# A routed feed-forward layer on one core: two-slot loops, weight pieces spread over four slots, row loads moved from SP to POOL

## The reference

```python
x = x + jnp.tanh(g_xattn[0]) * xattn(ctx_512, layernorm(x), W, b)   # 0.6*sigmoid(si+sj+b) + 0.4*layernorm(x)
# ffn: xt = layernorm(x) as (4096, 1024); W is (8, 1024, 1024), b is (8, 1024)
logits = xt @ wg
probs = jax.nn.softmax(logits, axis=-1)
idx = jnp.argmax(probs, axis=-1)
gate = jnp.take_along_axis(probs, idx[:, None], axis=1)
expert_out = jnp.einsum('nh,eoh->neo', xt, W) + b[None, :, :]
out = jnp.einsum('ne,neo->no', one_hot(idx) * gate, expert_out)
x = x + jnp.tanh(g_ffn[0]) * out
```

## Time and profile before

| | us |
|---|---|
| median of 3 runs | 683.54 |
| lowest, highest | 682.17, 690.35 |
| span of the profiled execution | 687.3 |

### The profile page before, as it was taken

How to read it: one execution, slowest core, us unless ns; L and a number is a source line. 1 busy time by engine, 2 the same in 40 slices (tenths; PEclk the granted TensorE clock), 3 DMA queues, 4 the chain that set the end, 5 groups by cost and what they waited for, 6 DMA issues and landing times.

```text
span 687.3 us, 14019 instructions
## 1 busy us (share of the span) xinstructions
PE 576.6 (84%) x2841; PEld 461.2 (67%) x2842; DVE 445.2 (65%) x557; ACT 274.1 (40%) x408; POOL 331.8 (48%) x489
## 2 busy tenths in 40 slices
PE   7898889888707969979779997995999799699990
PEld 5576667666505848858567885884888588588870
DVE  3357778697699885856784587588378557843420
ACT  2367766686424333413333333333343233333220
POOL 1446777788623336325336533633633364356540
PEclk8569999999957989989989998997999899899995
DMA  7911577576679876764776497577756656545530
GB/s 262 403 40 33 175 261 237 198 217 223 239 258 259 238 214 190 225 208 152 224 220 196 147 243 213 189 219 215 217 168 204 189 166 198 164 132 186 182 126 13
DMA packets 83666, 134.72 MB, mean 196 GB/s; under 512 B 11568, under 2 KB 64304, under 8 KB 83504
## 3 DMA queue, kind: packets, MB, share of 16 engines
q1 hardware_dynamic: 73712, 99.47, 49.4%
q0 software_dynamic: 9792, 33.82, 12.8%
HBM read 99.44 MB, written 35.91 MB: 197 GB/s over the span
## 4 chain that ended last, share of the span: by engine, by line
PE 27%; DVE 23%; issue 19%; ACT 9%; POOL 7%; DMA 6%; DVEq 3%; POOLq 2%; ACTq 2%; SPq 1%
PE pair L1058 12%; DVE wt L782 7%; PE pair L985 4%; DVE xr L718 4%; ACT wt L598 4%; DVE pair L777 4%; PE pair L996 3%; PE pair L969 3%; PE pair L974 3%; ACT rb L617 2%; DVE rows L804 2%; DMA out_x<-rows,scatter_row 2%; DMA rows<-table 1%; DVE xc_tr L725 1%; POOL out_x L500 1%
## 5 line engine op out<-in xcount | busy, mean ns | idle before, releaser
L1058 PE MATMUL pair<-wt,xt 128*128 x1728 | 416.2, 404 | 62.6 <-DVE rows L804 41.6
L1058 PEld LDWEIGHTS pair<-wt,xt 128*128 128x128 f32 x1728 | 336.9, 196 | 141.5 <-issue 66.5
L488 POOL TENSOR_TENSOR rows<-rows,rb 128x1024 f32<-128x1024 f32 x37 | 88.7, 2398 | 164.2 <-ACT rb L617 162.6
L782 DVE TENSOR_TENSOR wt<-pair,wt 128x1024 f32 (+1 forms) x64 | 77.5, 1212 | 32.7 <-ACT wt L598 32.7
L598 ACT ACTIVATE wt<-pair 128x1024 f32 (+1 forms) x64 | 64.2, 1024 | 77.7 <-DVE pair L777 70.1
L604 ACT ACTIVATE xt<-pair 128x1024 fp32r<-128x1024 f32 x38 | 39.0, 1026 | 133.0 <-DVE pair L790 110.6
L777 DVE STREAM_TRANSPOSE pair<-w_raw 128x1024 f32<-128x1024 f32 x64 | 79.7, 1250 | 1.9
L790 DVE STREAM_TRANSPOSE pair<-xb 128x1024 f32<-128x1024 f32 x38 | 47.7, 1255 | 46.5 <-issue 26.3
L804 DVE SCALAR_TENSOR_TENSOR rows<-pair,scal,rows 128x1024 f32<-128x1024 f32 x36 | 46.0, 1278 | 44.6 <-PE pair L1058 44.2
L617 ACT ACTIVATE rb<-bias_bc,scal 128x1024 f32 (+1 forms) x37 | 46.0, 1244 | 48.4 <-POOL scal L485 41.1
L794 DVE TENSOR_TENSOR xt<-pair,xt 128x1024 fp32r<-128x1024 f32 x38 | 46.4, 1221 | 28.1 <-ACT xt L604 25.9
(11 more groups left out here) (123 smaller groups left out, 417.9 us busy)
## 6 DMA issues: line engine op xcount, KB each, us to landing
w_raw<-in_L_ffn_W SPq DMA_DIRECT2D x256, 128.0 KB
xb<-table SPq DMA_DIRECT2D x156, 128.0 KB
rows<-table SPq DMA_DIRECT2D x38, 520.0 KB
xr<-in_x SPq DMA_DIRECT2D x32, 512.0 KB, 6.9
ctx_in<-in_ctx SPq DMA_DIRECT2D x8, 512.0 KB, 4.9
bias_bc<-in_L_ffn_b SPq DMA_DIRECT2D x8, 512.0 KB
out_x<-rows,scatter_row POOLq DMA_INDIRECT x36, 4.2
table<-xr,pos POOLq DMA_INDIRECT x32, 4.5
```

Of the source, the lines that this page charges most:

```text
L488: nc.gpsimd.tensor_tensor(rows[:, k, 0:H], rows[:, k, 0:H], rb[:, :], ALU.add).then_inc(base_ready, 1)
L782: nc.vector.tensor_tensor(where[:, :, 1].rearrange("p a k o -> p (a k) o"), ps[:, :].rearrange("p (k o) -> p k o", k=K), where[:, :, 0].re ...
L1058: last = nc.tensor.matmul(out_ps[r % 2][:, HALF * h:HALF * (h + 1)], xt[:, r % RING, x_part, k, :], wt[:, bass.ds(par, 1), w_part, k, HALF ...
```

## The change

- The slot loops of SP, ACT and DVE hold two slots in place of six and run 21 times; POOL's holds three (`RING`) and runs 14 times. PE's stays at six.
- Weight pieces are prepared in pairs: one pair in each of an expert's first four slots (if an expert had fewer, its last slot would take the rest). `slot_tab` row 3 is now the number of the pair, row 0 is 1 plus the number of pairs of the slot. One text with registers (`turn_pair`, `pair_low`, `pair_high`) serves all.
- `w_raw` has three buffers; in the loop two are used, and each is loaded again as soon as it is turned (`behind_pair`).
- In ACT's slot `exp_sum` stands behind the weight pieces.
- The plain rows are loaded by POOL, in `slot_scalars` ahead of its wait for `esum_ready`, and POOL itself waits there for `out_stored` of slot t-1.
- Ahead of the loop, with three buffers, piece m of expert 0 waits for piece m-3 to be turned, not m-4. The tables take DVE 11 small operations where there were 7.
- At the end POOL also waits for the last weight loads.

```diff
-    WR = 4
+    WR = 3
...
-                        load_rows(sp, row_of(t + 2), r + 2)
...
+            def behind_pair(m):
+                after = sp.snap((m + 1) % (E * PAIRS))
+                for n in range(2):
+                    sp.wait_ge(w_turned, 2 * m + n + 1)
+                    load_next(2 * after + n, n)
...
-            def slot_scalars(u, n, k):
+            def slot_scalars(u, n, k, meanwhile):
...
                 nc.gpsimd.tensor_tensor(scal[:, k, 3:4], scal[:, k, 1:2], rows[:, k, MEAN:MEAN + 1], ALU.add)
+                meanwhile()
                 settled(esum_ready, u + 1)
...
+                    def rows_behind(t=t, r=r, i=i):
+                        row0 = pool.value_load(slot_tab[0:1, 2, bass.ds(t + 2, 1)], min_val=0, max_val=E * N - P)
+                        if r:
+                            settled(out_stored[r - 1], 16 * i + 16)
+                        else:
+
+                            with pool.If(i > 0):
+                                settled(out_stored[RING - 1], 16 * i)
+                            with pool.Else():
+                                pool.nop()
+                        load_rows(pool, row0, r + 2)
...
+            def pair_high(m):
+                par = act.snap((m // PAIRS) % 2)
+                column = act.snap((m % PAIRS) * (2 * P))
+                for n, ps in enumerate((cut_b, cut_a)):
+                    act.wait_ge(w_turned, 2 * m + n + 1)
...
+                        with dve.If(work > 1):
+                            m = dve.value_load(slot_tab[0:1, 3, bass.ds(t, 1)], min_val=PAIRS, max_val=E * PAIRS - 1)
+                            turn_pair(m, 0, cut_b)
+                            xt_low(t + 2, home, cut_a)
+                            dve.wait_ge(xt_ready, t + 3)
+                            turn_pair(m, 1, cut_a)
+                            pair_low(m, 0, cut_b)
+                            pair_low(m, 1, cut_a)
+                            settled(w_ready, 2 * m + 2)
```

More of the change, by code:

```diff
@@ L630, in _ @@
             act.wait_ge(slots_told, 1)
[L631 to L647 removed]
+            with act.Fori(0, SLOTS // 2) as i:
+                for r in range(2):
+                    t = 2 * i + r
+                    work = act.value_load(slot_tab[0:1, 0, bass.ds(t, 1)], min_val=0, max_val=MOST)
@@ new lines, in _ @@
+            with dve.Fori(0, SLOTS // 2) as i:
+                for r in range(2):
+                    t = 2 * i + r
+                    work = dve.value_load(slot_tab[0:1, 0, bass.ds(t, 1)], min_val=0, max_val=MOST)
+                    with dve.If(work > 0):
+                        dve.wait_ge(xt_ready, t + 2)
+                        turn_rows(t + 2, i + 1, r, cut_a)
+                        home = dve.snap((t + 2) % RING)
+                        with dve.If(work > 1):
[7 more added lines that the diff above has]
+                            settled(w_ready, 2 * m + 2)
+                            with dve.If(work > 2):
+                                with dve.Fori(0, MOST - 2) as n:
+                                    more = dve.snap(work - n)
+                                    with dve.If(more > 2):
+                                        m1 = dve.snap(m + n + 1)
+                                        turn_pair(m1, 0, cut_b)
+                                        turn_pair(m1, 1, cut_a)
+                                        pair_low(m1, 0, cut_b)
+                                        pair_low(m1, 1, cut_a)
+                                        settled(w_ready, 2 * m1 + 2)
+                                    with dve.Else():
+                                        dve.nop()
```

243 lines of the change are left out of this document (111 added, 132 removed).

## The result

The changed kernel takes 647.84 us in the median of 4 runs (642.14 to 648.85), the kernel before 682.86 us (679.1 to 690.35) in the same comparison. The ratio is 0.949, with a 95% interval of 0.941 to 0.957: 35 us less, faster by 5%. The forecast was 667, that is 16.5 less. Direction and range were right; the change in time was sized at less than half of what it is. In all that follows medians and ranges count every execution and ratios only the fast ones (within 1.5% of the kernel's fastest), and the profiles of after_again and rows_on_sp are of executions that were not fast.

A forecast was written before the change was run, and what follows sets the result against it. The prediction took POOL's closed cycle, 12.2 us per slot, as the new bound: first store at 234.6, 35 more slots adding 427, then 9.4 at the end, span 671.0, 16.3 below the profiled 687.3, so 667 us; range 636 to 694.

The forecast's parts named there:

- DVE stops being the bound: Slot loop: spread pieces and late `exp_sum` bring DVE to 9.6 us per slot, under PE's 11.0.
- a closed cycle of POOL: Slot loop: store issued, landed, row load issued, L481 to L488, next store; at 12.2 us POOL becomes the bound.
- Two signs of the forecast: PE in the loop: idle 1.2 us in every slot, and `finish` waiting for POOL rather than for PE.
- the sum for POOL's cycle: POOL per slot: 5.3 store to row load, 1.07 issue, 0.2 to next operation, 5.6 to next store; 12.2 us.
- between this and the forecast: POOL cycles of 11.3 to 11.8 us, 636 to 653 us in all, counted to the forecast's mechanism.
- The end: From the last store to the program's end: 9.4 us remain of 15.9, 6.5 saved by shorter unused slots.
- The rival that PE stays the bound: Slot loop: POOL's cycle stays under PE's 11.0 us per slot, giving 622 us; chance 0.12.
- The late `exp_sum`: ACT's slot: with `exp_sum` behind the pieces, DVE's 3.0 us wait for ACT in a heavy slot goes.
- The return of a branch: Loop ends: rival that short-text returns cost as much as now, every second slot; 698 us, or 667 to 673; chance 0.08.
- Late stores: Rival: weight loads in 28 slots delay store landings; at 6.2 us the cycle is 13.1, 698 us; chance 0.15.
- The way into the loop: Ahead of the loop: piece 7 waits for the fifth turn, so PE starts 3.8 us later, at 215.0.
- The clock: PE in the loop: short idling of 1.2 us per slot costs no clock, so nothing was charged.

The follow-up runs named there:

- after_again: The changed kernel itself, run again unaltered in the second group of experiments: 641.67 us, ratio 0.934 to the kernel before.
- rows_on_sp: Changed kernel with the row loads and their store wait back on SP, SP's text again six slots: 657.64 us, ratio 0.945 to the kernel before.
- late_load: Changed kernel with POOL's store wait and row load moved behind the gate chain, ahead of the wait for `rb`: 633.71 us, ratio 0.912 to the kernel before.
- pool_longer: Changed kernel with one more POOL operation, a 128x512 fill behind the row load, in every slot: 655.04 us, ratio 0.948 to the kernel before.
- bursts: Changed kernel with four pieces in each of an expert's first two slots, none in the next two: 735.01 us, ratio 1.065 to the kernel before.
- exp_early: Changed kernel with `exp_sum` back ahead of the weight pieces on ACT: 686.06 us, ratio 0.994 to the kernel before.
- before_rows_on_pool: Kernel before with only the row loads moved to POOL, ahead of the gate chain: 723.87 us, ratio 1.051 to the kernel before.
- long_text: Changed kernel with the slot loops of SP, ACT and DVE written out for six slots again: 656.18 us, ratio 0.952 to the kernel before.
- before_both: Kernel before with `exp_sum` behind the weight pieces and row loads on POOL: 694.75 us, ratio 1.010 to the kernel before.
- late_load_four: Changed kernel with the row load behind the gate chain and four weight buffers ahead of the loop: 628.6 us, ratio 0.911 to the kernel before.
- before_exp_late: Kernel before with only `exp_sum` moved behind the slot's weight pieces on ACT: 673.4 us, ratio 0.975 to the kernel before.

## Why the prediction was right or wrong

**DVE stops being the bound: right.** PE has no wait for `finish` in the changed kernel's profile where it had 41.6 us.

**The mechanism, a closed cycle of POOL: right.** It is in the timeline, late_load took its wait off the path and gained 14 us, pool_longer lengthened it and lost 10. The stores are at equal distances over heavy and light slots, POOL's largest wait is the row load's for the store, and `rb` waits for L487, as was said.

**What the cycle does to PE: wrong.** Two signs of the forecast didn't come: PE was to idle 1.2 us in every slot, and `finish` was to wait for POOL. PE idled 2.95 us in all, in two gaps, one of them over 2 us. L843, the start of `finish`, came 0.4 us behind L490 in the eight light slots only; in the 28 heavy ones it came 5.0 to 9.0 us behind it, after DVE's own low parts. At 11.23 the cycle is only 0.18 us above the 11.05 of a free PE (late_load), 6 us over the loop, and PE's lead of up to two slots can take that up. POOL's cycle shows at the end instead: the last store starts 11.2 us behind PE's last matmul.

**The size of the cycle: wrong, and this is the main miss.** The step that failed is the sum for POOL's cycle, 5.3 + 1.07 + 0.2 + 5.6 = 12.2. The means over all slots are:

| term | forecast | measured |
|---|---|---|
| store start to row load start | 5.3 | 4.80 (3.56 to 5.69) |
| issue of the row load on POOL | 1.07 | 0.63 |
| to the next operation | 0.2 | 0.03 |
| L483 to the next store | 5.6 | 5.8 |
| cycle | 12.2 | 11.23 |

Over 35 slots the 0.97 us are 34 us. Two terms make most of it, and both had been taken high. The store's 5.3 was the old mean of 5.2 with something added, because a weight load would run beside nearly every store. The opposite came: a store lands in 3.9 us in the median and 4.9 at most, against 4.2 and 6.8, and the row load starts 0.8 us behind the landing. It is tempting to credit the spreading, but the runs don't bear that out. Medians of 3.5 to 3.9 stand in bursts, exp_early, pool_longer and before_rows_on_pool as well, of which two have bursts; rows_on_sp, which is spread, has 4.5, late_load 4.6, long_text 4.3, before_both 4.4. What sets a store's landing time within 3.5 to 4.6 us stays open. The issue was priced by the only POOL issue in the trace, an indirect one. A plain load costs POOL 0.63 us, and the middle between the two bounds of the forecast (0.35 and 1.07) was 0.71. The prediction chose the row with the same engine as the likeness; the kind of transfer counted as much.

With 11.23 the kernel lies at the lower edge of what the prediction put "between this and the forecast", and close to PE's 11.0. That the range of 636 to 694 held is in part luck: by the prediction's own sum a cycle of 11.23 gives 633 us, and the earlier first store 3 less. The end, 6.9 us longer than forecast, and a median that lies 7 us above the profiled span, where the forecast took it 3.8 below, brought the time back inside. The rival that PE stays the bound (622 us) is the one that late_load_four comes nearest to with 628.6.

**What each part is worth: wrong in two places.** The late `exp_sum` was counted as 3.0 us of a heavy slot. Alone it is 17 us of the kernel (before_exp_late), but without it the rest of the change is worth 4 (exp_early): `finish` then falls behind POOL's L490, and POOL's cycle takes it in. The prediction's sum used the late order and so did not suffer, but it didn't see that nearly the whole gain hangs on this order. And of the short texts it said that their return is hidden behind POOL's cycle. long_text shows 13 us for long ones, 0.45 us per slot, of which 0.13 are seen as waits for a return's delay. The 0.3 us of a return itself was right (0.25 to 0.38 us on the four engines).

**The rule of the Trainium skill on a transfer from GpSimd (DMA: Bandwidth & Descriptors, "Anatomy of one DMA — SWDGE (gpsimd) path").** The prediction set its 3.2 us, and a cycle near 11.1, against the rows. Its figure for the transfer was again too low: 3.9 us in the median for a store and 4.6 for a row load. Its cycle came out near the 11.23 by luck, since the issue and the 0.2 us behind it had been taken too high beside it.

**The return of a branch (Runtime: NRT & Kernel Launch, "Instruction fetch mechanics").** The rival said that a short text may still pay at the window's edge. The trace refutes the rival, not the page: all 73 returns of DVE, ACT, POOL and SP in the changed kernel take 0.25 to 0.38 us, while those of DVE's long text in long_text take 2.8 to 5.1 us.

**Late stores: refuted.** The longest flight is 4.9 us, and 6.3 and 5.3 in the two repeats, against 6.8 before; the median is 3.9 in all three.

**The way into the loop: the wait is there, its sum was not needed.** DVE waited 5.99 us for the blocks of slot 0 where it had waited 0.82, and PE's idle time ahead of the loop grew from 20.9 to 27.05. The forecast's 3.8 us are 4.4 by late_load and late_load_four. But the first stage ended some 5 us earlier in this execution, so PE started at 211.0, as before, and not at 215.0. In the nine profiles with the changed way in PE started between 205.2 and 217.7.

**The end: wrong.** 9.4 us were forecast from the last store, 16.3 came. Up to POOL's last operation the forecast holds (7.3 us against 7.1). Of the 9.4 it named 5.0 and 0.2, 1.2 and 2.3 us, 8.7 together, and gave no number for the rest, the store's landing. What it did not know is that POOL's DRAIN of 8.7 us follows. Before, 5.6 us of it ran beside DVE's unused slots and ended with them, and so the forecast's chain of the end named DVE and not POOL. It rests on the loop's returns of DVE and POOL, and on no row of the program's last lines.

**The bookkeeping.** In spans: 35 x 0.97 = 34 us less for the cycle, 3.4 less for the first store (231.2 against 234.6), 6.9 more for the end, together 30.5 less than the 671.0 of the forecast; the trace has 30.4. In medians the miss is 19, since this profile was its kernel's fastest execution.

**The clock: right, and worth more than was said.** In the two stretches that cover most of the loop the granted clock is 1.00, the 2.4 GHz level as in the earlier trace rows:

```profile
252.00:400.00 148.00, 148.00 (x649) 121.43 (x648) 108.34 (x102) 59.13 (x77) 81.56 (x131) 1.00 0.78 232
400.00:600.00 200.00, 197.05 (x860) 161.11 (x859) 131.35 (x124) 73.92 (x98) 113.00 (x180) 1.00 0.71 215
```

(stretch, length, busy us of PE, PEld, DVE, ACT and POOL with counts, clock, DMA share, GB/s). Here PE idled too little to try the forecast's 1.2 us. exp_early does: its PE idled 19 times for `finish`, up to 1.8 us at a time, and from 400 to 600 us the clock stayed at 1.00 (first row). In the kernel before, with gaps of 4 to 7 us, it was 0.93 (second row):

```profile
400.00:600.00 200.00, 179.33 (x768) 143.16 (x766) 146.81 (x119) 69.80 (x92) 100.07 (x160) 1.00 0.69 200
400.00:600.00 200.00, 179.46 (x751) 145.28 (x749) 138.50 (x120) 69.83 (x90) 86.63 (x136) 0.93 0.68 200
```

The loop's matmuls took 399.1 us of PE after and 416.2 before. So of the 55.7 us that PE's part of the loop became shorter, 39 are idle time and 17 are the clock behind the gaps.

## What to carry to other kernels

When a wait is moved into a closed cycle of an engine, the sum of the cycle decides, and if it comes within a microsecond of the next bound, each term is worth its own bound: a mean with a guess on top is not one, and the issue of a plain and of an indirect transfer are two prices. Put such a wait where the engine waits anyway; here that took 14 us more, with one line moved. Parts of a change that all touch one cycle are not worth a fixed amount each, so read in the timeline what comes right behind each moved operation on every engine before it is priced, and read the program's last lines for what is hidden there.

## What the runs showed of the hardware

- POOL's DRAIN at the end takes 5.63 us in the kernels whose row loads are SP's (before, before_exp_late, rows_on_sp), and 8.73 us in the eleven others, all with 38 plain loads from POOL beside 68 indirect stores. It is the same within 0.01 us in each of the two groups. Two runs tried it, one in each direction: rows_on_sp took the loads from POOL and had 5.63, before_rows_on_pool gave them to POOL in the old kernel and had 8.73. By what way the loads lengthen it stays open.
- A DVE operation of 0.16 us on one column took up to 2.3 us and ended with a running POOL operation on 128x1024, 27 times of 27 (exp_early).
- Issue on POOL: 0.63 us for a plain load of 520 KB, 1.08 for an indirect store of 512 KB, in the same slots.
- Executions of the changed kernel differ by 12 us in when PE starts in the loop (205.2, 211.0 and 217.7 us), more than the 4.4 us that the third buffer there costs; only PE's idle time before the loop shows those.
